# A graph network's edge sort on one core: target search by accumulating operations, attribute pieces on GpSimd, 16 of 26 one-hots on ScalarE, blank records stored one stage earlier

## What is computed

```
edge_index = stack([src, dst])                     # edges come sorted by dst, not by src
x = x + hyperbolic_block(relu(layernorm(x)), edge_index, W)          # sums per node edge[0]
h = relu(layernorm(x))
e = concat([h[src], h[dst], edge_attr])            # edge_attr: 4 numbers per edge
msg = bn_relu(bn_relu(e @ Wm1 + bm1) @ Wm2 + bm2)  # batch norm over all edges
u = concat([h, segment_sum(msg, src)])
x = x + bn_relu(bn_relu(u @ Wu1 + bu1) @ Wu2 + bu2)
```

## Time and profile before

| | |
|---|---|
| Median of 3 runs | 17072.78 us (17068.78 to 17084.48) |
| Profiled execution | 17093.01 us, of which 17091.3 us span |
| Node stage (barrier to barrier) | 26 to 290 us |
| Counts | 290 to 404 us |
| Sort loop with its tail | 404 to 3304 us |
| All that follows | 3304 to 17091 us |
| VectorE busy, whole span | 8652.0 us (51%) |
| GpSimd busy, whole span | 9635.6 us (56%) |

### The profile page before, as it was taken

How to read it: one execution, slowest core, us unless ns; L and a number is a source line. 1 busy time by engine, 2 the same in 40 slices (tenths; PEclk the granted TensorE clock), 3 DMA queues, 4 the chain that set the end, 5 groups by cost and what they waited for, 6 DMA issues and landing times. The chain is left out here.

```text
span 17091.3 us, 195568 instructions
## 1 busy us (share of the span) xinstructions
PE 6354.3 (37%) x50077; PEld 5035.1 (29%) x50078; DVE 8652.0 (51%) x18303; ACT 4054.6 (24%) x7861; POOL 9635.6 (56%) x9968
## 2 busy tenths in 40 slices
PE   2444444311111111111159522323223223258996
PEld 2444444300000000000058511111111111125995
DVE  5888888623333333333268733333333333346884
ACT  1666666400000000000058400000000000024333
POOL 0555555466656665666657356666666666622773
PEclk7777777655555555555579756655655656579998
DMA  2000000133323332323444222222222222275331
GB/s 58 8 8 8 8 8 8 27 75 75 75 66 73 75 74 68 74 69 74 67 106 151 67 66 66 68 63 68 67 65 68 65 66 68 65 145 187 106 107 54
DMA packets 1142331, 1160.59 MB, mean 68 GB/s; under 512 B 688769, under 2 KB 832769, under 8 KB 1142018
## 3 DMA queue, kind: packets, MB, share of 16 engines
q1 hardware_dynamic: 845634, 680.39, 13.9%
q0 software_dynamic: 235008, 248.13, 8.6%
q10 hardware_dynamic: 61632, 231.44, 3.4%
HBM read 872.56 MB, written 286.75 MB: 68 GB/s over the span
## 5 line engine op out<-in xcount | busy, mean ns | idle before, releaser
L1559 POOL DMA_INDIRECT big<-b_d,big x3424 | 3284.0, 959 | 2270.7 <-POOLq L144 1232.2
L1084 POOL DMA_INDIRECT big<-h_d,big x3424 | 3273.9, 956 | 2001.9 <-issue 1189.0
L1145 DVE TENSOR_REDUCE ps<-ps 128x260 f32<-128x780 f32 x856 | 837.8, 979 | 3275.1 <-remote 1441.1
L1126 PE MATMUL ps<-big 128*128 x3424 | 737.9, 373 | 4609.0 <-issue 3388.5
L1686 DVE TENSOR_REDUCE ps<-ps 128x256 f32<-128x768 f32 x856 | 827.6, 967 | 2582.9 <-DVEq L144 1605.9
L1126 PEld LDWEIGHTS ps<-big 128*128 128x128 bf16 x3424 | 442.4, 162 | 4904.3 <-issue 4901.1
L1638 PE MATMUL ps<-big 128*128 x3424 | 608.7, 335 | 2615.9 <-issue 2130.1
L1885 POOL TENSOR_SCALAR big<-iota_f,big 128x128 f32<-128x128 f32 x1498 | 880.4, 608 | 827.7 <-DMA big<-rec_d 528.3
L1638 PEld LDWEIGHTS ps<-big 128*128 128x128 bf16 x3424 | 444.6, 160 | 2973.7 <-issue 2973.7
L777 ACT ACTIVATE big<-big 128x512 bf16<-128x512 bf16 x1736 | 1076.7, 708 | 907.1 <-ACTq L144 907.1
L1092 ACT ACTIVATE big<-big 128x16 int32<-128x16 f32 x214 | 49.1, 229 | 4899.9 <-issue 2304.5
(11 more groups left out here) (409 smaller groups left out, 14488.7 us busy)
## 6 DMA issues: line engine op xcount, KB each, us to landing
big<-e_d SPq DMA_DIRECT2D x428, 512.0 KB, 3.1
rows_d<-big ACTq DMA_DIRECT2D x214, 544.0 KB
big<-rows_d SPq DMA_DIRECT2D x214, 544.0 KB, 3.2
HA<-slots_d SPq DMA_DIRECT2D x214, 512.0 KB
big<-slots_d SPq DMA_DIRECT2D x214, 512.0 KB
e_d<-big ACTq DMA_DIRECT2D x214, 512.0 KB
big<-rec_d SPq DMA_DIRECT2D x860, 64.0 KB, 2.9
big<-h_d,big POOLq DMA_INDIRECT x3424
```

What stands on the lines that cost most here:

```text
L1084: gp.indirect_dma_start(G[g][:, t * ROW:(t + 1) * ROW], None, h0_d, bass.IndirectOffsetOnAxis(idx[g % 2][:, t:t + 1], 0)).then_inc(gath[g] ...
L1126: m = t.matmul(XS[q % 2][:, n, 0:3 * D + 3], OT3[g % 2][:, o, :], T0[:, ds(chunks[o // 2] * TW, 3 * D + 3)], start=True, stop=True)
L1145: v.tensor_reduce(xrow[:, q * QT:(q + 1) * QT, :], XS[q % 2][:, :, 0:3 * D + 3].rearrange("p t (q w) -> p t w q", q=3), AX, ALU.add).then_ ...
L1559: gp.indirect_dma_start(G[g][:, t * D:(t + 1) * D], None, b_d, bass.IndirectOffsetOnAxis(idx[g % 2][:, t:t + 1], 0)).then_inc(gath[g], 16)
```

## The change

What it does, in seven points:

1. **Targets.** The three operations on 4x100 numbers (685, 687, 688) become four `scalar_tensor_tensor` of 100 numbers, one for each group of 128 segments: comparison with `g8[:, w]`, product with `STEP`, and the sum in `accum_out`.
2. **Attribute pieces.** `attributes` leaves VectorE; GpSimd does the same five operations at the start of `spread`, ahead of the wait for `l_rdy`. The semaphores `pa_rdy` and `pa_free` are gone.
3. **One-hots.** `ACTD` goes from 14 to 16: VectorE makes 10 of 26, ScalarE 16.
4. **Wait for the casts.** The wait for `s_cast` of 5 moves from ahead of the loop on VectorE to just ahead of the first supertile's one-hots, and to ScalarE's and GpSimd's own streams.
5. **Blank records.** `blank` lies at the end of `big` and is filled in the first block; its stores are issued in the node stage, after the edge loads, and waited for at that stage's end.
6. **Order in the node stage.** The two `wblk` loads are issued ahead of the edge loads.
7. **Counts.** `LO` (64 columns) becomes the weights, `HI` (104 columns) the moving side; the few operations behind it are turned accordingly.

```diff
@@ node stage
             def _(sp):
+                sp.wait_ge(s_w, 1)
+                for h in range(2):
+                    sp.dma_start(wblk[h * D:(h + 1) * D, h * D:(h + 1) * D], w0t).then_inc(s_st, 16)
                 for t_, a_ in ((s_i, src), (d_i, dst)):
                     sp.dma_start(t_[0:P - 1, :], ...).then_inc(s_edges, 16)
                     sp.dma_start(t_[P - 1:P, 0:LASTE], ...).then_inc(s_edges, 16)
-                sp.wait_ge(s_w, 1)
-                for h in range(2):
-                    sp.dma_start(wblk[h * D:(h + 1) * D, h * D:(h + 1) * D], w0t).then_inc(s_st, 16)
+                sp.dma_start(rec_d.rearrange("(k p t) w -> p k (t w)", p=P, t=TB),
+                             blank.unsqueeze(1).to_broadcast([P, NBLK + 2, TB * REC])).then_inc(s_blank, 16)
+                sp.dma_start(rec2_blk[NBLK:NBLK + 2].rearrange("k p w -> p k w"),
+                             blank.unsqueeze(1).to_broadcast([P, 2, TB * REC])).then_inc(s_blank, 16)
                 sp.wait_ge(s_v, 82)
                 sp.dma_start(h0_d.rearrange("(c p) w -> p c w", p=P), ROWS).then_inc(s_st, 16)
                 sp.wait_ge(s_st, 48)
                 sp.wait_ge(s_edges, 64)
+                sp.wait_ge(s_blank, 32)
@@ counts
-                        last = t.matmul(joint2, HI[b][:, m:NHI * w:step], LO[b][:, m:NLO * w:step], ...
+                        last = t.matmul(joint2, LO[b][:, m:NLO * w:step], HI[b][:, m:NHI * w:step], ...
@@ sort
-        ACTD = 14
+        ACTD = 16
...
-                v.wait_ge(s_cast, 5)
...
                     if not last:
                         flags(1 - b, s + 1)
+                    if first:
+                        v.wait_ge(s_cast, 5)
                     for j in range(J - ACTD):
                         n = go(v.tensor_scalar(DH[b][:, j * WS:(j + 1) * WS], iota_w, seg_f[b][:, j:j + 1], None, ALU.is_equal))
                     need(n)
                     v.sem_inc(d_rdy, 1)
                     if not last:
                         before(1 - b, s + 1)
-                        attributes(1 - b)
                     need(go(v.tensor_tensor(ANC[:, 1:NC + 1], gpos[b], INC[:, 0:NC], ALU.subtract)))
                     need(go(v.tensor_tensor(STEP, ANC[:, 1:NC + 2], ANC[:, 0:NC + 1], ALU.subtract)))
-                    need(go(v.tensor_tensor(hit3, INC.unsqueeze(1).to_broadcast([P, NW, NC + 1]),
-                                            g8.unsqueeze(2).to_broadcast([P, NW, NC + 1]), ALU.is_le)))
-                    need(go(v.tensor_tensor(hit3, hit3, STEP.unsqueeze(1).to_broadcast([P, NW, NC + 1]), ALU.mult)))
-                    need(go(v.tensor_reduce(dsum, hit3, AX, ALU.add)))
+                    for w in range(NW):
+                        n = go(v.scalar_tensor_tensor(out=hit3[:, w, :], in0=INC, scalar=g8[:, w:w + 1], in1=STEP,
+                                                      op0=ALU.is_le, op1=ALU.mult, accum_out=dsum[:, w:w + 1]))
+                    need(n)
                     go(v.tensor_tensor(dest[b], dsum, g8, ALU.add))
@@ gpsimd
+                def attributes(b):
+                    consume(gp, att_in[b], 32)
+                    a3 = attb[b].rearrange("p (j a) -> p j a", a=4)
+                    r3 = rem.rearrange("p (j a) -> p j a", a=4)
+                    gp.tensor_copy(PA[b][:, :, 0, :], a3).then_inc(s_piece, 1)
+                    gp.wait_ge(s_piece, 1)
+                    gp.tensor_tensor(r3, a3, PA[b][:, :, 0, :], ALU.subtract).then_inc(s_piece, 1)
+                    gp.wait_ge(s_piece, 2)
+                    gp.sem_inc(att_free[b], 1)
+                    gp.tensor_copy(PA[b][:, :, 1, :], r3).then_inc(s_piece, 1)
+                    gp.wait_ge(s_piece, 3)
+                    gp.tensor_tensor(r3, r3, PA[b][:, :, 1, :], ALU.subtract).then_inc(s_piece, 1)
+                    gp.wait_ge(s_piece, 4)
+                    gp.tensor_copy(PA[b][:, :, 2, :], r3).then_inc(s_piece, 1)
+                    gp.wait_ge(s_piece, 5)
+                    gp.sem_inc(s_piece, -5)

                 def spread(b, s):
+                    attributes(b)
                     consume(gp, l_rdy)
-                    consume(gp, pa_rdy)
                     consume(gp, e_free[b])
```

85 lines of the change are left out of this document (34 added, 51 removed).

## The result

On the chip of the first runs the kernel after takes 16636.62 us (median of 4 runs, 16630.78 to 16642.91) against 17070.78 before (4 runs, 17068.22 to 17084.48): ratio 0.9744, 95% interval 0.9727 to 0.9761, or -434 us. The direction and the mechanism are as forecast. The time lies 3 us under the lower end of the range and 70 us under the forecast of 16707, so one or more terms of the sum were mis-sized.

The account below looks back on a forecast made before the run. VectorE's chain in the sort loop was taken as the bound. From the profiled 17093: loop -270, tail +2, node stage -63, counts -27, casts -8 give 16727; less 20 to the median, 16707 us, range 16640 to 16850.

Parts of the forecast that it names:

- VectorE's chain sets the period: Sort loop: VectorE runs without real pauses, so its own chain sets the 23.20 us period; 21.0 us after the change.
- Targets, -0.75: Sort loop: four accumulating operations take 1.08 us instead of 1.83 on VectorE, -0.75 us per period.
- One-hots, -0.65: Sort loop: two fewer one-hots on VectorE at 0.324 us each, -0.65 us per period.
- Pieces, -1.56 and +0.75 for blocking: Sort loop: attribute pieces leave VectorE, -1.56 us; on GpSimd they block VectorE by some two fifths of 1.8 us, +0.75.
- The ring at 20.8: Sort loop: VectorE's release, spread, `place`, `ranks` and hand-over take 20.8 us; VectorE savings beyond 2.4 us are lost.
- Rival 1: Sort loop: the ring bounds, engines slip past each other (VectorE +0 to +0.4); period 20.8, -295 us, 16682; chance 0.2.
- Node stage, -63: Node stage: with the weight loaded ahead of the edge lists the chain moves by -63.4 us, table's store at 203.2.
- the blank store hides: Node stage: the blank store ends at 201, 2 us before the table's store, so costs nothing; if late, gain only -25.
- Counts, -27: Counts: 64 instead of 104 weight columns at two cycles each make 403 pairs 0.123 us instead of 0.1893, -27 us.
- The bound of 0: Counts: if a strided moving column costs two cycles too, 104 of them bound at the old 0.19 us, gain 0.
- Casts, -8: Before the sort loop: VectorE's 7.67 us wait ahead of its first flags falls behind 11 us of other work, -8 us.
- The later stages, 0: Stages behind the sort: no changed instructions, so the remaining 13,787 us are taken as they are.

Follow-up runs that it names:

- b_pieces: Kernel before with only the five attribute-piece operations moved from VectorE to GpSimd at the start of `spread`; period 21.80 us, -1.40.
- a_early: Kernel after with VectorE's release of the spread matmuls (`l_rdy`) moved right behind the copy that makes `n8`; 14873.9 us, period 20.32 us.
- a_early_nopieces: a_early with GpSimd's five attribute-piece operations left out of every supertile, the pieces zeroed once; 14845.2 us, period 20.12 us.
- c_both: a_early with 17 one-hots on ScalarE and both sides of the counting matmuls contiguous; 16575.35 us, ratio 0.9712 to the kernel before.
- c_hi: a_early with 17 one-hots on ScalarE and only the counts' 104 moving columns contiguous, written element by element; first supertile starts at 363.7 us.
- b_order: Kernel before with only the two weight loads issued ahead of the edge lists; 15229.6 against 15283.79 us, period 23.18 us.

## Why the prediction was right and where it was wrong

- **VectorE's chain sets the period: right**, in both kinds of period. Every us taken off came back: -2.69 by single parts, -2.73 together.
- **Targets, -0.75: right**, measured -0.74.
- **One-hots, -0.65: too much**, measured -0.55. The busy time of the group divided by 12 was taken, which spreads over all of them what three lose beside GpSimd's indirect DMAs; a short one's step in the chain is 0.27.
- **Pieces, -1.56 and +0.75 for blocking: the step that failed.** The take-off was right, the blocking measured a net 0.16 (b_pieces) and 0.19 us (a_early against a_early_nopieces). The overlap in time was foreseen exactly, and wrongly turned into a price: a share of two fifths had no row behind it, nor had its reason, that the fixed part of an operation needs no port. The difference, 0.56 to 0.59 us over 123 periods, is about 70 us; the one-hots take 12 of it back. With 0.11 for the one-hots and a blocking of 0.19 to 0.26 us the chain comes to 20.24 + 0.30 to 0.37 = 20.54 to 20.61 us. L649 (L662 before) and the loop's turn gave 0.1 and 0.05 us that the sum had not, which makes 20.39 to 20.46, where 20.42 to 20.47 was measured.
- **The ring at 20.8: too long.** It was read from one supertile (20.61) with 0.2 us added for the hand-over. The median over the loop before is 20.46 us, and in the kernel after it is 20.2 on the first chip and 19.1 on a 15300 one; the shortest hand-over seen is 0.15. Rival 1 had two halves. That the engines slip past each other (VectorE +0 to +0.4) was right; that the ring then bounds at 20.8 was not, and priced it 41 us too dear at a period of 20.47.
- **Node stage, -63: right.** The first transpose came at 88.34 and the store at 203.34, both as forecast. That the blank store hides was right, with more room than the 2 us given. SP's queue was free at 118.84 + 71.94 = 190.8, and the 15 engines that don't carry the edge lists were done before 170 (from there on the share is 0.07, about one engine of 16):

```profile
88.34 1.73 PE L360 MATMUL ps<-ident,big 128*128 128x128 f32 x7 [88.34 <-DVE big L291]
```

```profile
118.84 71.94 SPq L268 DMA_DIRECT2D rec_d<-big  x1
203.34 0.37 SPq L271 DMA_DIRECT2D h_d<-big  x1
```

```profile
140.00:150.00 10.00, 2.30 (x12) 2.11 (x10) 7.42 (x2) 0.00 (x0) 0.00 (x0) 0.67 1.02 314
160.00:170.00 10.00, 0.00 (x0) 0.00 (x0) 8.19 (x26) 3.31 (x5) 0.00 (x0) 0.50 0.70 204
170.00:180.00 10.00, 0.00 (x0) 0.00 (x0) 9.93 (x3) 0.00 (x0) 0.00 (x0) 0.50 0.07 22
```

  The 2.7 us between the store's -63.2 and the counts' -60.5 are the time from the store to the barrier, 26.5 us here and 23.4 to 24.5 in nine other profiles that share this code (26.4 and 26.3 in c_both and c_hi, on one chip); b_order, without the blank store in that stage, had 24.1. So it is not the blank store's; what it is stays open.
- **Counts, -27: wrong**, measured 0 (76.3 us for 403 pairs, as the earlier trace rows). Two rows on a line through "two cycles a weight column" looked like proof, but the one was strided bf16 and the other contiguous f32, two different cases with one number; what binds the f32 pair isn't shown. The bound of 0 was stated, and with the right side of the matmul, though not with its reason: the price of a strided column is 1.8 ns at either clock and not two cycles.
- **Casts, -8: right**, -7: what is left of -67.4 after -60.5.
- **The later stages, 0: not quite.** -50 between the profiles, -33 against medians on that chip, -17 on the other 17000 chip where both were profiled, nothing on the 15300 chip. The cause isn't shown.

Against the profiled execution the sum was 16727 and the time 16642, 85 us less: -66 from the loop, +27 from the counts, +3 and +1 from barrier and casts, -50 from the later stages. Of the 85, 15 go in the step to medians, as the profiled execution of after lies 5 us above its median and not 20. That the forecast was no further off than 70 us is in part luck: the 27 us wrongly expected of the counts hid as much of the other errors.

## What to carry to other kernels

Two engines that can block each other at a shared port cost what their operations meet, not what their busy times overlap: here a tenth to a fifth of the block that was moved came back as blocking, not two fifths, and which operations meet changes with a shift of 0.8 us. When a price is fitted to two rows, see that both have the same type and the same step, and ask of each side of a matmul whether it is read side by side. Before a ring is called the bound, its length should be measured over many periods and in more than one profile: here its end lay 0.15 us ahead of the next supertile in one profile and 1.2 us in another, at the same period. An experiment that brings the expected number should still be asked for its mechanism.

## What the runs showed of the hardware

- A strided column of bf16 at a step of 124 bytes costs TensorE 1.8 ns on the longer strided side, weights or moving; seen at a granted clock of 0.50 for both sides and at 1.00 for strided weights, alike. Contiguous pairs of 64 and 104 columns take 0.087 us at 0.50 and 0.046 at 1.00.
- VectorE writes 496 bf16 one-hots in runs of 16 bytes as fast as side by side (0.284 us), and element by element at a step of 208 bytes at 1.49 us.
- An accumulating operation of 100 f32 with two SBUF sources takes 0.24 us back to back; GpSimd's small operations of 104 elements take 0.27 to 0.38 us.
- DMAs that use all 16 engines and one that sits on a single engine ran beside each other at 310 GB/s in all; the single one then trailed at 22 GB/s (before: 27).
- VectorE's one-hots of 512 bf16 last 0.33 to 0.36 us, and 0.54 to 0.58 when they span the end of one of GpSimd's indirect DMA operations.
- Chips differ by 10% for this kernel, all of it in stages of indirect gathers: 4350 against 5100 to 5212 us for the same 3424 gathers.
